# A Perceiver block on Trainium2: the feed-forward weights quantised during the key and value projections, from a turned layout, instead of during cross attention

## The reference

```python
x = x + L0_xattn(layernorm(x), ctx)      # 16 query heads, 4 key heads, head size 96
x = x + L0_attn(layernorm(x))            # causal
x = x + L0_ffn(layernorm(x))             # routed low-rank update
x = x + L1_xattn(layernorm(x), ctx)      # 32 query heads, 8 key heads, head size 32
x = x + L1_attn(layernorm(x))            # causal
x = x + L1_ffn(layernorm(x))
def L0_xattn(latents, context):
    hidden = concat([context, latents])   # 4352 rows
    k, v = hidden @ Wk.T, hidden @ Wv.T
    ...
def L1_ffn(x):                            # I = 2752
    def quant_w(W):                       # one scale a row of W
        ws = maximum(max(abs(W), axis=1) / 127, 1e-8)
        return clip(round(W / ws), -127, 127), ws
    q, s = quant_act(rmsnorm(x) * weight)
    gate = (q @ Wgq.T) * s * wsg.T        # Wg, Wu: 2752 x 1024
    up = (q @ Wuq.T) * s * wsu.T
    q2, s2 = quant_act(silu(gate) * up)
    return (q2 @ Wdq.T) * s2 * wsd.T      # Wd: 1024 x 2752
```

## Time and profile before

| | us |
|---|---|
| median of three runs | 2080.06 (2078.8 to 2082.45) |
| the profiled execution | 2078.95 |
| its span, first to last instruction | 2077.6 |
| TensorE busy in the span | 1922.5 (93%) |
| VectorE busy | 1282.2 (62%) |
| ScalarE busy | 859.6 (41%) |
| GpSimd busy | 546.3 (26%) |

### The profile page before, as it was taken

The page is one execution under the profiler, slowest core; times in us unless marked ns, Lnnn a source line. Parts: engine busy times, 40 slices in busy tenths (PEclk is TensorE's granted clock), DMA queues, the critical chain, the costliest instruction groups (busy, mean ns, idle before and its releaser), DMA issues.

```text
span 2077.6 us, 29638 instructions
## 1 busy us (share of the span) xinstructions
PE 1922.5 (93%) x11932; PEld 1412.7 (68%) x11932; DVE 1282.2 (62%) x1608; ACT 859.6 (41%) x1409; POOL 546.3 (26%) x264
## 2 busy tenths in 40 slices
PE   7899999999997999999999997889999999988977
PEld 5799999999996777777777786523333333366833
DVE  3444444545443788788976764767777775266455
ACT  2211111111112566656564452146777767635421
POOL 0000000000000555554520000136777777510000
PEclk9999999999998999999999999889999999999989
DMA  5533334343225766665634434633433320046052
GB/s 176 175 102 112 117 97 125 93 124 99 74 79 147 211 202 190 199 192 200 229 123 143 148 113 102 162 107 79 98 81 80 90 69 1 21 139 225 1 190 77
DMA packets 154808, 259.30 MB, mean 125 GB/s; under 512 B 36477, under 2 KB 102321, under 8 KB 147505
## 3 DMA queue, kind: packets, MB, share of 16 engines
q1 hardware_dynamic: 154673, 257.42, 41.3%
HBM read 192.39 MB, written 61.76 MB: 122 GB/s over the span
## 4 chain that ended last, share of the span: by engine, by line
PE 80%; DVE 10%; ACT 3%; DMA 3%; issue 2%; SPq 0%; POOL 0%; ACTq 0%; DVEq 0%
PE psum L476 11%; PE psum L1722 7%; PE psum L1739 5%; PE psum L457 4%; PE psum L459 4%; PE psum L458 4%; PE psum L444 4%; PE psum L285 3%; PE psum L286 3%; PE psum L287 3%; DVE top L1915 3%; PE psum L1755 3%; PE psum L1703 3%; PE psum L817 3%; PE psum L832 3%; PE psum L424 2%
## 5 line engine op out<-in xcount | busy, mean ns | idle before, releaser
L1915 DVE TENSOR_REDUCE top<-psum 128x4 f32<-128x2048 f32 (+1 forms) x146 | 294.0, 2025 | 98.0 <-PE psum L1703 97.8
L1985 POOL TENSOR_TENSOR added<-probs_f 128x1024 f32<-128x1024 f32 x126 | 299.0, 2374 | 164.9 <-ACT probs_f L1840 117.0
L1840 ACT ACTIVATE probs_f<-psum 128x512 f32<-128x512 f32 x512 | 278.4, 594 | 136.9 <-PE psum L1722 124.4
L609 DVE TENSOR_REDUCE top<-psum 128x2 f32<-128x512 f32 x272 | 186.4, 691 | 198.2 <-PE psum L444 198.0
L908 DVE TENSOR_TENSOR probs_low<-probs,probs_high 128x1024 fp32r<-128x1024 f32 x136 | 199.2, 1469 | 76.1 <-ACT probs L871 76.0
L870 ACT ACTIVATE probs_high<-psum 128x1024 fp32r<-128x1024 f32 x136 | 139.8, 1028 | 165.3 <-PE psum L819 149.4
L1722 PE MATMUL psum<-q_rows,k_rows 97*128 97x512 f32 x512 | 196.0, 457 | 2.5 <-DMA q_rows<-t_high 1.9
L1722 PEld LDWEIGHTS psum<-q_rows,k_rows 97*128 97x128 f32 x512 | 80.0, 189 | 171.2 <-ACT probs_f L1840 161.0
L457 PE MATMUL psum<-c_high,w_high 128*128 128x256 f32 (+1 forms) x672 | 190.7, 284 | 3.2 <-issue 3.2
L458 PE MATMUL psum<-c_low,w_high 128*128 128x256 f32 (+1 forms) x672 | 190.5, 284 | 0.0
L459 PE MATMUL psum<-c_high,w_low 128*128 128x256 f32 (+1 forms) x672 | 190.3, 283 | 0.0
(11 more groups left out here) (359 smaller groups left out, 3807.7 us busy)
## 6 DMA issues: line engine op xcount, KB each, us to landing
wf_rows<-in_ffn_w_dram SPq DMA_DIRECT2D x42, 512.0 KB, 4.2
staged<-in_ctxT_dram SPq DMA_DIRECT2D x32, 512.0 KB, 4.6
k_four<-k_high SPq DMA_DIRECT2D x128, 128.0 KB, 3.3
wf_rows<-in_ffn_w_dram SPq DMA_DIRECT2D x8, 1376.0 KB, 7.6
q_dram<-wf_turned SPq DMA_DIRECT2D x42, 256.0 KB, 2.2
gate_up<-q_dram SPq DMA_DIRECT2D x10, 1024.0 KB, 8.1
value_high<-v_high SPq DMA_DIRECT2D x32, 256.0 KB, 3.6
value_low<-v_low SPq DMA_DIRECT2D x32, 256.0 KB, 4.6
```

Of the source, the lines that this page charges most:

```text
L609: dve.tensor_reduce(top0[:, r0:r0 + 2, n], psum[:, bank, :].rearrange("p (i n) -> p i n", i=2), AX_X, ALU.max).then_inc(*b.bank_read.up())
L1840: act.activation(probs[:, n % 6, half * BANK:(half + 1) * BANK], psum[:, half, :], ACT.Exp, scale=scale).then_inc(*f.exped.up())
L1915: dve.tensor_reduce(top1[:, first:end, t, chunk], psum[:, MAXIMA + first:MAXIMA + end, :], AX_X, ALU.max).then_inc(*f.max_read.up())
L1985: pool.tensor_tensor(added[pair % 4][:], probs[:, n % 6, :], probs[:, (n + 1) % 6, :], ALU.add).then_inc(*f.added.up())
```

## The change

The quantisation leaves `cross_stage` and goes into `latent_stage`, and TensorE's turning of it is dropped. The host now also hands over the three weight matrices transposed (`ffn_t0`, `ffn_t1`, `ffn_t2`, f32), beside the row layout. The row layout is loaded only for the maxima, the turned one for rounding.

- **Slots.** Context chunks 1 to 15 get six slots each, each a "find" and a "settle" step within `chunk_steps`, placed by `SLOTS`. In slot i VectorE finds the maxima of row block i (68 blocks of up to 128 x 1024), with scale and inverse at the end of each block of up to 512 columns. The unit r = i - 18 (70 units of 128 x 2 x 512, turned) is rounded by ScalarE in two passes: add the constant, subtract it into bf16, in place. GpSimd has multiplied it by the inverses before that, as soon as it lands: one multiply by a row of 512 inverses that lies on all partitions. SyncE loads row block i + 3 and turned unit i - 16 at "settle" and stores unit i - 19 at "find".
- **Inverses** go to DRAM, transposed, 4 bytes an element, and come back broadcast over 128 partitions, once for each of 14 blocks.
- **Buffers.** The four turned buffers are one new tile, `staged[2]` and two halves of `xnT`; `staged[3]` holds the inverses. So chunk loads from chunk 1 on use only `staged[0]` and `staged[1]`, the latents go through DRAM (`xnT_dram`) for chunk 16, and `q_low` is no longer resident: the low queries lie in the second pair of chunk buffers, are stored to `q_low_dram`, and are loaded back before chunk 16. ScalarE waits for that store before it splits chunk 1.
- **Cross attention** loses its quantiser; the four units of output weights are split after steps 120, 124, 128 and 132.
- **Last stage.** `q_dram` is laid out by chunks of 512 columns, `qd_dram` by partition; chunk and `down` loads are long runs, and the ragged last chunk is multiplied 192 columns wide instead of 128 and 64.

```diff
+            turned += [staged[2][:, 0:2 * BANK], flat[:, 0:2 * BANK], flat[:, 2 * BANK:4 * BANK]]
+            inverses = [staged[3][:, i * BANK:(i + 1) * BANK] for i in range(2)]
...
+            q_low_parts = [z[1].rearrange("p k n -> p (k n)") for z in (c_high, c_low)]
...
+                z = i % 2 if what == "c" and i >= 2 else n % 4
...
+            blocks = [(0, 0), (1, 0), (2, 0), (0, 1), (1, 1), (2, 1)] + [(z, i) for i in range(2, chunks) for z in range(2)]
+            tops, top_end, pairs, pair_start = [], [], [], []
+            for z, i in blocks:
+                for tile in range(4 * i, min(4 * i + 4, KT if z == 2 else FT)):
+                    tops += [(z, tile, part) for part in range(3 if z == 2 else 1)]
+                top_end.append(len(tops) - 1)
+                pair_start.append(len(pairs))
+                pairs += [(len(top_end) - 1, z, i, m) for m in range((FT if z == 2 else KT) // 2)]
+            LAG = 17
...
+            SLOTS = {("mm", 0, 0, 0): "find", ("mm", 0, 0, 5): "settle", ("mm", 0, 1, 1): "find",
+                     ("mm", 1, 0, 0): "settle", ("mm", 1, 1, 0): "find", ("mm", 2, 0, 0): "settle",
+                     ("mm", 2, 0, 2): "find", ("vmm", 0, 0, 0): "settle", ("vmm", 0, 0, 3): "find",
+                     ("vmm", 1, 0, 0): "settle", ("vmm", 1, 0, 2): "find", ("vmm", 1, 0, 5): "settle"}
...
+                if n == 1:
+                    act.wait_ge(*b.q_low_sent.at(32))
...
+                def settle(r):
+                    z = width_of(*pairs[r][1:3])
+                    wide = turned[r % 4][:, 0:2 * z]
+                    act.wait_ge(*b.scaled.at(r + 1))
+                    act.activation(wide, wide, ACT.Copy, bias=ROUND).then_inc(*b.shifted.up())
+                    act.wait_ge(*b.shifted.at(r + 1))
+                    act.activation(turned[r % 4].bitcast(BF16)[:, 0:2 * z], wide, ACT.Copy,
+                                   bias=-ROUND).then_inc(*b.rounded.up())
...
+                        if what == "settle" and 0 <= i - LAG - 1 < len(pairs):
+                            settle(i - LAG - 1)
...
+                    dve.wait_ge(*wf_in[m % 3].at(16 * (m // 3 + 1)))
+                    dve.tensor_reduce(top, rows[m % 3][0:height, 0:cols], AX_X, ALU.max,
+                                      apply_absolute_value=True).then_inc(*b.topped.up())
...
+                for r, (block, z, i, m) in enumerate(pairs):
+                    width = width_of(z, i)
+                    both = turned[r % 4][:, 0:2 * width].rearrange("p (z n) -> p z n", z=2)
+                    if m == 0:
+                        pool.wait_ge(*b.inverse_in.at(16 * (block + 1)))
+                    pool.wait_ge(*wt_in[r % 4].at(16 * (r // 4 + 1)))
+                    pool.tensor_tensor(both, both, inverses[block % 2][:, 0:width].unsqueeze(1).broadcast_to([P, 2, width]),
+                                       ALU.mult).then_inc(*b.scaled.up())
...
+                def load_turned(r):
+                    _, z, i, m = pairs[r]
+                    width = width_of(z, i)
+                    if r >= 4:
+                        sp.wait_ge(*spilled[r % 4].at(16 * (r // 4)))
+                    elif r == 1:
+                        sp.wait_ge(*b.w_split.at(KT))
+                        sp.wait_ge(*b.q_made.at(H0))
+                        sp.wait_ge(*b.c_split.at(2))
+                    elif r == 2:
+                        sp.wait_ge(*b.xnT_sent.at(32))
+                    sp.dma_start(turned[r % 4][:, 0:2 * width].rearrange("p (z n) -> p z n", z=2),
+                                 turned_place(a[f"ffn_t{z}"].rearrange("(k p) n -> p k n", p=P), z, i, m)).then_inc(
+                                     *wt_in[r % 4].up(16))
...
+                        if what == "find":
+                            if 0 <= i - LAG - 2 < len(pairs):
+                                spill(i - LAG - 2)
+                        elif what == "settle":
+                            if i + 3 < len(tops):
+                                load_rows(i + 3)
+                            if i in top_end:
+                                send_inverses(top_end.index(i))
+                            if i - LAG + 2 in pair_start:
+                                load_inverses(pair_start.index(i - LAG + 2))
+                            if 0 <= i - LAG + 1 < len(pairs):
+                                load_turned(i - LAG + 1)
...
-                    for what, m, first, last in quant[n]:
-                        if what == "turn":
-                            turn(m, first, last)
...
+            width = min(BANK, FF - i * BANK)
             for which in range(2):
-                first = which * FT + 4 * i
-                tile, flag = gate_up[i % 2][:, which, :], chunk_in[i % 2]
-                sp.dma_start(tile[:, 0:whole * KT * P].rearrange("p (i m) -> p i m", i=whole),
-                             q_dram[first:first + whole].rearrange("i p m -> p i m")).then_inc(*flag.up(16))
-                if whole < n:
-                    rest = lambda z: z.rearrange("p (k n) -> p k n", n=P)[:, :, 0:FF % P]
-                    sp.dma_start(rest(tile[:, whole * KT * P:n * KT * P]),
-                                 rest(q_dram[first + whole])).then_inc(*flag.up(16))
+                tile = gate_up[i % 2][:, which, 0:KT * width].rearrange("p (k n) -> p k n", n=width)
+                sp.dma_start(tile, q_dram[which, i, :, :, 0:width]).then_inc(*chunk_in[i % 2].up(16))
```

More of the change, by code:

```diff
@@ L347, in latent_stage @@
             phase = ExitStack()
+            rows = [sb(phase, f"wf_rows{i}", [P, D]) for i in range(3)]
+            turned = [sb(phase, "wf_turned", [P, 2 * BANK])]
+            parts = sb(phase, "wf_parts", [P, 2, 4, 3])
             xnT = sb(phase, "xnT_ab", [P, KT, T])
```

378 lines of the change are left out of this document (162 added, 216 removed).

## The result

The changed kernel takes 2093.16 us (median of five runs, 2089.9 to 2097.01); the kernel before takes 2080.06 (five runs). The ratio is 1.0063, with a 95% interval of 1.0046 to 1.0079: slower by 13 us. The forecast was 2072: a gain of 7 us where a loss of 13 came, so it is wrong by its sign, though 2093 lies inside the stated range of 2040 to 2110. The profiled execution took 2092.1 us, its span is 2090.8, against 2077.6 before.

A forecast was written before the change was run, and what follows sets the result against it. TensorE was taken as the bound, with 80% of the chain of waits. 2078.95 - 42 (cross attention) + 34 (DMA) + 2 (start) - 1 (last stage) = 2072 us; stated range 2040 to 2110, the forecast's own 2057 to 2086.

The forecast's parts named there:

- Part 1: Cross attention: removing 528 transposes from TensorE, with some waits and clock drops, saves about 42 us, bounds 37 and 46.
- Part 2: Key and value stage: the added work on VectorE, ScalarE and GpSimd fits within 33.9 us a chunk, costing 0.
- Part 3: Key and value stage: overlapped streams need 38.3 us of DMA a chunk, 4.4 over the period: loss about 34 us.
- Part 4: Start: ScalarE waits for the low queries' store, +2 us; their reload 0; last stage's longer load runs, -1 us.
- (b): Key and value stage, slots 19 to 64: DMA falls under 305 GB/s, giving 2086 to 2125 us; chance 0.26.
- (a): Key and value stage: DMA keeps up, chunks within 0 to 2.5 us of 33.9, giving 2038 to 2057; chance 0.22.
- (c): Cross attention: the gain isn't had, something else holds the step at 3.1 us, giving 2114 us; chance 0.02.
- a DMA share near 1.0: Key and value stage, from the fourth context chunk for about eight: expected at 300 to 330 GB/s, periods of 38 us.

The follow-up runs named there:

- the floor: Changed kernel without search, multiply, rounding, their loads and scales; the 70 unit stores stay, from a constant: 2037.1 us, 0.979, stage 530.1 us.
- the spreading: Changed kernel with inverses turned on VectorE and low queries in free buffers, plus row blocks searched five in three slots at first, then two: 2082.7 us, 1.0011.

## Why the prediction was wrong

**Part 1, cross attention (-42): right**, -44.7, within its bounds of 37 to 46. The stage takes 383 us where about 385 was said, and TensorE's waits in it are 6.2 us; about 8 us are left over the 374.4 of clean steps, where the part left 11.

**Part 2, compute fits: right as to the engines**, shown by the kernel with turned scales and no row loads: it searches, multiplies and rounds everything and is 3 to 6 us above the floor. Two terms were small: the multiply takes 2.45 us instead of 2.37, and VectorE's low parts beside it cost more than before (last section), which the part had at nothing.

**Part 3, the DMA engines (+34): here the prediction failed**, at the sentence "The scales add about 0.4 MB a chunk, as each block's row of 512 inverses is broadcast over 128 partitions." It counted the loads of the broadcast and gave the 14 stores that come before them no price. They cost 30.5 us of the stage. The term that the part did work out was too large: with turned scales the stage is 556.3 - 532.3 = 24 us longer than before, where 34 was said. The eight slow periods have a mean of 37.0 instead of 38.3; the rate in them is 313 GB/s, just that of the working (12.0 MB in 38.3 us), but a chunk moved 11.6 MB instead of 12.0. That the rate fits is in part luck: the part took the bytes for the cause, and the spreading shows that they alone don't set the period. Together 24 + 30.5 = 54.5, the whole difference. With both terms at the size measured, the sum would have been 2072 - 10 + 30 = 2092; the errors of the other parts (+3.3, +1.1, -2.0, -2.7) cancel, which is luck.

The kernel before has no store of this form, but the change's own flag on it, `allow_slow_non_contiguous`, was there to be read, and no bounds were set for it. The Trainium skill's rule of 512 bytes was in the same table as the figure of memory bandwidth that the prediction quoted.

**Part 4:** start +2 with bounds 0 and 4, measured +5.3: the store of the low queries took 9.86 us instead of 5, and a key eviction that TensorE needs stood behind ScalarE's wait, as the part said. The way to cross attention took 1.1 more. Last stage -1 with bounds 0 and 3: from its first product to the end it takes 76.8 us instead of 80.4, so -3.6, over the bound. TensorE's waits for gate and up fell from 4.3 to 2.2 us, the longest from 1.64 to 1.27, and a load of 1 MB lands in 6.9 us instead of 8.1. The other 1.5 us weren't followed up.

**Rivals.** (b), slower from a period of 39.3 us on, is what came: 40.0, with the engines at a share of 1.03 and 292 GB/s, under its 305. Its reason wasn't there: strided runs of 2 KB were its main argument, and long runs changed nothing. That its number came true is luck. (a) is refuted for this kernel, with a period of 40.0 and, without the 4-byte stores, of 37.0, over its 36.4; (c) by the steps of cross attention. Of the signs named in the prediction, "a DMA share near 1.0" came true and would have been read as bytes; it took the run without row loads, 229 GB/s at a share of 0.94, to see that it wasn't bytes alone.

**Open:** why a second store right behind the first costs half; why the packets behind such a store take microseconds; whether piece size or number of pieces matters; by what path the row loads cost their 16 to 23 us, bytes or the lateness of a unit; and the last 3 to 6 us above the floor.

## What to carry to other kernels

Count the packets of each new DMA beside its bytes: in this kernel a store with pieces of 4 bytes was worth turning on an engine first, and it cost nothing where the DMA engines had slack. A DMA share near 1 is a symptom; set GB/s beside it in windows of 2 to 4 us, and look at what SyncE issued just before the rate falls. Removing one stream of bytes and removing the odd transfer are two experiments that cost one edit each, and they should both come before any reordering.

## What was unexpected of the hardware

- Behind a store of 512 pieces of 4 bytes the rate of all transfers falls for some 8 us, while the share stays near or over 1: to 207 GB/s on average over 12 stores in the busy stage (310 with the data turned so that a piece has 128 bytes), and to 10 to 200 in the quiet one, in windows of 2 us. The small packets take 8 to 17 ns on average; some others near them take up to 5.5 us.
- The engines reached 388 to 406 GB/s in windows of 4 us with a single core at work. The prediction weighed the Trainium skill's 358 GB/s for a core ("DMA: Bandwidth & Descriptors", Specifications); these windows are above it, and the measurement decides. Over 200 us the best was 314, with shares of 0.94.
- VectorE's subtraction for the low part took 1221 ns before the change and 1745 now, beside GpSimd's multiplies; the maximum, with one input, takes 1210, before 1205. The groups, from 115 to 700 us:

```profile
L753 POOL TENSOR_TENSOR xnT_ab<-xnT_ab,staged 128x1024 f32<-128x1024 f32 x30 | 73.5, 2451 | 151.8 <-DMA xnT_ab<-in_ffn_t_dram 151.7
L563 DVE TENSOR_TENSOR c_low<-staged,c_high 128x1024 fp32r<-128x1024 f32 x30 | 51.2, 1745 | 0.9
L649 DVE TENSOR_REDUCE w_top<-wf_rows 128x1 f32<-128x1024 f32 x42 | 50.3, 1210 | 2.4 <-DMA wf_rows<-in_ffn_w_dram 2.4
```

By the Trainium skill, "SBUF — State Buffer", section "SBUF: two separate sides", a VectorE operation with two SBUF inputs and a GpSimd operation take a shared pair of ports in turn, each for its whole instruction. The trace agrees; here VectorE has time to spare, and what it costs lies within the 3 to 6 us above the floor.
